# A two-layer attention and expert kernel: first operands chunk by chunk, chunks in natural order, three score banks, routing inside the loop, gathers in smaller groups

## What is computed

```python
# layer 0: s = linear attention by running sums, g = x @ ternary weights + bias
# layer 1 attention (16 heads of 16), over all rows of its batch, causal:
qkv = hidden_states @ qkv_w.T + qkv_b
scores = einsum('bqhd,bkhd->bhqk', q, k) * scale + slope[h] * (key - query)
attn = softmax(where(key <= query, scores, NEG))
out = (attn @ v) @ out_w.T + out_b
# layer 1 experts: the best 2 of 8 for each row
logits = x @ gate_w.T + gate_b
top_vals, top_idx = top_k(logits, 2); routing = softmax(top_vals)
for e in range(8):
    h = x @ w1[e].T + b1[e]
    y = h[:, 0::2] * sigmoid(1.702 * h[:, 0::2]) * (h[:, 1::2] + 1)
    out += (y @ w2[e].T + b2[e]) * weight_of(e)
```

## Time and profile before

| what | value |
|---|---|
| median of 3 runs | 972.3 us (968.9 to 974.0) |
| profiled execution, its own time | 969.48 us |
| its span, first to last instruction | 967.7 us |
| mean granted TensorE clock | 0.923 |
| PE, DVE, ACT, POOL busy | 796.4, 635.3, 498.7, 313.9 us |

### The profile page before, as it was taken

One profiled execution on the slowest core, in us unless ns is written; L12 is line 12 of the kernel. 1 busy time (PEld: TensorE's weight loads), 2 busy tenths in 40 slices (PEclk: granted clock), 3 DMA queues, 4 the chain that ended last, 5 costly groups with the idle time before them and its releaser, 6 DMA issues.

```text
span 967.7 us, 13783 instructions
## 1 busy us (share of the span) xinstructions
PE 796.4 (82%) x4910; PEld 387.1 (40%) x4910; DVE 635.3 (66%) x1197; ACT 498.7 (52%) x1030; POOL 313.9 (32%) x363
## 2 busy tenths in 40 slices
PE   4474659914889999999999999999999995888986
PEld 1242345403324444444544444444444432222543
DVE  5999997665856666676566667666666763984121
ACT  2343315861555565555555655555565552556340
POOL 2766963121660060051006005100600516340111
PEclk9797979966799999999999999999999997999795
DMA  9501302332223235225223532522353112111110
GB/s 322 173 0 66 109 22 87 131 108 70 102 93 88 67 99 100 76 63 107 62 66 103 101 73 65 106 62 66 98 108 71 40 49 77 45 55 68 42 34 33
DMA packets 72392, 80.03 MB, mean 83 GB/s; under 512 B 33561, under 2 KB 56020, under 8 KB 72196
## 3 DMA queue, kind: packets, MB, share of 16 engines
q1 hardware_dynamic: 67660, 68.84, 26.0%
q0 software_dynamic: 3296, 8.62, 2.9%
q10 hardware_dynamic: 1368, 1.70, 0.6%
HBM read 34.22 MB, written 26.74 MB: 63 GB/s over the span
## 4 chain that ended last, share of the span: by engine, by line
PE 55%; DVE 26%; issue 7%; POOL 3%; DMA 3%; ACT 3%; SPq 1%; POOLq 0%; ACTq 0%; DVEq 0%
PE bank L1466 14%; DVE PM L1163 11%; PE bank L1424 10%; PE bank L1444 7%; PE bank L1361 5%; PE bank L1371 5%; PE bank L1481 3%; DVE PR L960 3%; PE bank L1256 2%; PE bank L1508 2%; DMA OPS<-qk_parts 2%; DVE YT L1062 2%; POOL XT L580 1%; POOL x_rows L569 1%; PE bank L1427 1%
## 5 line engine op out<-in xcount | busy, mean ns | idle before, releaser
L1163 DVE TENSOR_REDUCE PM<-bank 128x1 f32<-128x512 f32 (+3 forms) x640 | 368.6, 605 | 217.7 <-PE bank L1427 160.1
L811 ACT ACTIVATE PR<-bank 128x512 f32<-128x512 f32 (+3 forms) x640 | 331.6, 536 | 302.7 <-PE bank L1447 150.7
L1424 PE MATMUL bank<-OPS 108*128 108x512 bf16 (+3 forms) x640 | 228.5, 361 | 72.3 <-DVE PM L1163 36.1
L1444 PE MATMUL bank<-OPS 111*128 111x512 bf16 (+3 forms) x640 | 225.0, 354 | 3.3 <-ACT PR L811 3.1
L1466 PE MATMUL bank<-PR,VS 128*17 128x512 f32 (+3 forms) x1280 | 159.0, 548 | 0.5 <-ACT PR L811 0.4
L540 POOL TENSOR_TENSOR NP<-NM,NIL 128x8 bf16<-128x8 f32 x32 | 6.5, 202 | 429.9 <-DVE NM L1171 429.8
L1424 PEld LDWEIGHTS bank<-OPS 108*128 108x128 bf16 x640 | 64.2, 100 | 193.3 <-DVE PM L1163 131.9
L1361 PE MATMUL bank<-WB 128*128 128x256 f16 x552 | 90.7, 272 | 0.0
L527 POOL TENSOR_TENSOR OPS<-POSR,SCL 12x2048 bf16<-12x2048 bf16 x24 | 87.8, 3680 | 7.6 <-PE bank L1447 7.6
L1444 PEld LDWEIGHTS bank<-OPS 111*128 111x128 bf16 x640 | 63.3, 99 | 39.0 <-ACT PR L811 15.6
L1361 PEld LDWEIGHTS bank<-WB 128*128 128x128 f16 x552 | 49.5, 99 | 44.6 <-issue 22.3
(11 more groups left out here) (187 smaller groups left out, 975.8 us busy)
## 6 DMA issues: line engine op xcount, KB each, us to landing
qk_parts<-OPS SPq DMA_DIRECT2D x16, 384.0 KB, 3.6
OPS<-qk_parts SPq DMA_DIRECT2D x32, 192.0 KB
x_rows<-PR SPq DMA_DIRECT2D x23, 256.0 KB, 3.6
WB<-W1H SPq DMA_DIRECT2D x23, 256.0 KB, 2.4
WB<-W1L SPq DMA_DIRECT2D x23, 256.0 KB, 2.4
WB<-in_w SPq DMA_DIRECT2D x23, 256.0 KB, 2.7
y_rows<-XT SPq DMA_DIRECT2D x23, 256.0 KB, 2.2
OPS<-qk_parts SPq DMA_DIRECT2D x32, 128.0 KB
```

The costliest lines, as they stand in the source:

```text
L811: act.activation(PR[:, tile % RING, off:CH], PS[2 + tile % 2][:, off:CH], ACT.Exp).then_inc(b_exped, 1)
L1163: dve.tensor_reduce(PM[:, c % 2, j, xq, gg:gg + 1], bank[:, 0:width], AX.X, ALU.max).then_inc(a_reduced, 1)
L1424: last = mm(bank[:, 0:width], OPS[0:ROWS_A, h % 4, 0, P * (TC * a + xq):P * (TC * a + xq) + P], OPS[0:ROWS_A, h % 4, 1, CH * gg:CH * gg + ...
L1444: last = mm(bank[:, off:CH], OPS[0:ROWS_B, h % 4, 1, P * k:P * k + P], OPS[0:ROWS_B, h % 4, 0, CH * b + off:CH * b + CH], start=True, stop ...
```

## The change

The chunk order becomes 0, 1, 2, 3, with 8, 16, 24 and 32 tiles: a pair's chunks end at places 7, 23, 47 and 79, and every turn comes five steps later (places 12, 28, 52, 4). The parts of queries and keys move to memory outside the operand region OPS, and SP stores each chunk and then loads that chunk of heads 0 and 1 (twelve transfers a chunk) instead of loading whole rows at the end; heads 2 and 3 stay as they were. Before PE's first tile of a chunk in pair 0 there is now a wait for that chunk alone. The position rows of heads 0 and 1 move from ACT to POOL, ahead of the last two experts' weight scaling. The ranking becomes five operations on 1024 elements a partition, and the whole routing (36 operations, two a step) runs in steps 1 to 18 of the loop, the turning of the weights and the bias products in steps 19 to 41. After the first 44 tiles the first pass uses three banks (0, 1, 6), and PE waits for the reduction of tile n - 3. Both halves of `up` use bank 5: the second half starts nine steps after the first and waits for DVE's reading of the first; `down` comes 18 steps after the start, blocks start at step 92. The scatters go in groups of 4, 8 and 4 tiles, the gathers in groups of 3, 5 and 8. POOL's list around `rows` is not touched.

```diff
-ORDER = (0, 3, 1, 2)
+ORDER = (0, 1, 2, 3)
-FIRST_BLOCK, EVERY = 84, 20
+FIRST_BLOCK, EVERY = 92, 20
-TURN_AT = {chunk_end(m) - 1 + (3, 4, 5, 3)[m % NC]: m for m in range(NC * PAIRS)}
-HEADS_AT = {chunk_end(m) - 1 + LEAD + (15, 11, 11, 11)[m % NC]: m for m in range(NC * PAIRS)}
+TURN_AT = {chunk_end(m) - 1 + 5: m for m in range(NC * PAIRS)}
+HEADS_AT = {chunk_end(m) - 1 + LEAD + 11: m for m in range(NC * PAIRS)}
-DOWN_AT = {n + 14: b for n, b in BLOCK_AT.items()}
+DOWN_AT = {n + 18: b for n, b in BLOCK_AT.items()}
+BIAS_AT = {19 + 2 * k: k for k in range(NC + NT // 2)}
...
-            load(0)
-            load(1)
+            for c in range(NC):
...
+                sp.wait_ge(parts_out[0], 16 * c + 16)
+                sp.wait_ge(parts_out[2], 16 * c + 16)
+                for h in range(2):
+                    for side in range(2):
...
+                            sp.dma_start(OPS[row:row + rows, h, side, cols], src).then_inc(first_in[c], 16)
...
+            rows(0)
+            rows(1)
+            scale(E // 2 - 1)
+            pool.wait_ge(w1l_done, E - 2)
+            low_parts(E // 2 - 1)
...
-            scatter(range(0, 5))
+            scatter(range(0, 4))
             maxima(1)
-            scatter(range(5, 11))
+            scatter(range(4, 12))
             maxima(2)
-            scatter(range(11, NT))
+            scatter(range(12, NT))
             maxima(3)
...
-                    gather(0, GATHERS)
+                    gather(0, 3)
                 maxima(NC * p)
                 if p == PAIRS - 1:
-                    gather(GATHERS, 11)
+                    gather(3, 8)
                 maxima(NC * p + 1)
                 if p == PAIRS - 1:
-                    gather(11, NT)
+                    gather(8, NT)
                 if 1 <= p < PAIRS - 1:
                     pool.wait_ge(b_scored, PER_PAIR * p)
                     rows(2 * p + 2)
...
-                    if b == 0:
-                        pe.wait_ge(slots_done, 2)
-                    else:
-                        pe.wait_ge(y_ready, 2 * b + f - 1)
+                    wait(pe, y_ready, 2 * b + f)
-                last = mm(PS[5 + f][:, SLOTS * part:SLOTS * part + SLOTS], W1B[b % 2][:, wp, col:col + P],
+                last = mm(PS[5][:, SLOTS * part:SLOTS * part + SLOTS], W1B[b % 2][:, wp, col:col + P],
...
+                if p == 0 and tile == OFF[c]:
+                    pe.wait_ge(first_in[c], 16 * 12)
...
-                    pe.wait_ge(a_reduced, tile - 1)
-                bank = PS[tile % 4] if tile < WIDE else PS[tile % 2]
+                    pe.wait_ge(a_reduced, tile - 2)
+                bank = PS[tile % 4] if tile < WIDE else PS[(0, 1, 6)[tile % 3]]
```

The new ranking, first of 36 operations of `sort(k)`, two of which DVE does after each reduction:

```diff
+                if k == 0:
+                    ins = dve.tensor_tensor(RIVAL, other, own, ALU.is_gt)
+                elif k == 1:
+                    ins = dve.tensor_tensor(EQUAL, other, own, ALU.is_equal)
...
+                elif k == 4:
+                    ins = dve.tensor_reduce(RANK, RIVAL, AX.X, ALU.add)
...
+                if 1 <= n <= SORTED // 2:
+                    sort(2 * n - 2)
+                    sort(2 * n - 1)
```

More of the change, by code:

```diff
@@ L351, in _ @@
                 sp.dma_start(x1_dram[:, TC * c:TC * c + TC, :], XO[:, TC * c:TC * c + TC, :]).then_inc(x1_spill, 16)
-            with sp.Fori(0, NC) as c:
-                for m in range(4):
-                    side, half = m // 2, m % 2
-                    sp.wait_ge(qk_p2, 4 * c + m + 1)
-                    sp.dma_start(parts[side, :, half * P:half * P + P, ds(c * CH, CH)].rearrange("j f t -> f j t"),
-                                 QP[:, m, :, :]).then_inc(parts_out[m], 16)
             def load(h):
@@ L378, in rows_out @@
                         "j (q t) -> j q t", q=TC), MT[3 * TC * j:3 * TC * j + 3 * TC, m % 2, :]).then_inc(mrow[m % NC], 16)
-            for m in range(4):
-                sp.wait_ge(parts_out[m], 16 * NC)
-            load(0)
-            load(1)
+            for c in range(NC):
+                cols = slice(CH * c, CH * c + CH)
+                for m in range(4):
+                    side, half = m // 2, m % 2
+                    sp.wait_ge(qk_p2, 4 * c + m + 1)
+                    sp.dma_start(parts[side, :, half * P:half * P + P, cols].rearrange("j f t -> f j t"),
+                                 QP[m]).then_inc(parts_out[m], 16)
+                sp.wait_ge(parts_out[0], 16 * c + 16)
+                sp.wait_ge(parts_out[2], 16 * c + 16)
+                for h in range(2):
+                    for side in range(2):
+                        row = POS
+                        for first, parts_of, times_of in LOADS[side]:
+                            rows = HD * parts_of * times_of
+                            src = parts[side, first:first + parts_of, HD * h:HD * h + HD, cols]
+                            if times_of > 1:
+                                src = src.broadcast_to([times_of, HD, CH])
+                            sp.dma_start(OPS[row:row + rows, h, side, cols], src).then_inc(first_in[c], 16)
+                            row += rows
             sp.wait_ge(memset_done, 11)
@@ L387, in _ @@
                              ONEB[0:3, :].unsqueeze(1).broadcast_to([3, NC, CH])).then_inc(ones_in, 16)
+            for m in range(4):
+                sp.wait_ge(parts_out[m], 16 * NC)
             load(2)
@@ L721, in _ @@
                     wait(act, parts_out[m], 16 * c)
-                    act.activation(QP[:, m, 0, :], QV[:, m, :], ACT.Copy).then_inc(qk_p0, 1)
+                    if c == 0 and m == 2:
+                        act.wait_ge(x1_add, 2 * NC)
+                    act.activation(QP[m][:, 0, :], QV[:, m, :], ACT.Copy).then_inc(qk_p0, 1)
                 if c + 1 < NC:
@@ L746, in gate_linear @@
                 half = slice(SLOTS * f, SLOTS * f + SLOTS)
[L747 removed]
+                act.activation(GT[:, b % 2, half], PS[5][:, 0:SLOTS], ACT.Identity,
                                bias=BB[:, b % 2, 0, f:f + 1]).then_inc(gate_read, 1)
@@ L1117, in slots @@
-            def slots(k):
-                if k == 0:
-                    dve.wait_ge(count_ps, 1)
-                    dve.wait_ge(table_in, 16)
-                    dve.wait_ge(we_done, 2)
-                else:
-                    dve.wait_ge(chain, k)
-                if k == 0:
+            over = TMP.rearrange("p t e -> p (t e)")[:, 0:8 * E].rearrange("p (e j) -> p e j", e=E)
+            own = LG[:, :, :].unsqueeze(3).broadcast_to([P, NT, E, E])
+            other = LG[:, :, :].unsqueeze(2).broadcast_to([P, NT, E, E])
@@ L1403, in output_biases @@
                     tile = 2 * r + q
-                    last = mm(PS[4 + r % 2][:, D * q:D * q + D], WET[:, P * tile:P * tile + P], B2[:, :],
+                    last = mm(PS[4 + r % 2][:, D * q:D * q + D], WET[0:E, P * tile:P * tile + P], B2[0:E, :],
                               start=True, stop=True)
@@ L1512, in _ @@
             pe.wait_ge(cast_in, 32)
-            side_work = [(turn_routing, c) for c in range(NC)] + [(output_biases, r) for r in range(NT // 2)]
             for n in range(STEPS):
@@ L1516, in _ @@
                     score_a(n)
-                    if n % 2 and n // 2 < len(side_work):
-                        stage, which = side_work[n // 2]
-                        stage(which)
-                if n == 1:
+                    if n in BIAS_AT:
+                        if BIAS_AT[n] < NC:
+                            turn_routing(BIAS_AT[n])
+                        else:
+                            output_biases(BIAS_AT[n] - NC)
+                if n == 5:
                     count_tokens()
```

247 lines of the change are left out of this document (124 added, 123 removed).

## The result

The changed kernel takes 995.9 us (median of 4, 993.9 to 999.6) where the kernel before takes 972.8 (median of 4, 968.9 to 974.0): a ratio of 1.025, 95% interval 1.021 to 1.029. It is slower by 23 us. The forecast was 1013 us, slower, with a range of 988 to 1038: the side and the range held, the size was 17 us too large. The profiled execution took 993.9 us with a span of 992.1, against 969.5 and 967.7 before.

The account below looks back on a forecast made before the run. In-order PE bounds the loop and its waits are paid in full. Stalls +52, clock +18, banks and gate work -5, start -10, gathers -12, tail +0.5 make +43.5 on 969.5: 1013 us, range 988 to 1038.

Parts of the forecast that it names:

- the main step: Turn at place 52, pairs 1 to 6: PE waits 8.7 us a pair for POOL's unchanged list, 52 us in all.
- The rival with the loads: Third chunk's maxima at place 68, behind next pair's loads: some 5 us late, hidden by the stall at place 52; 4%.
- The 995 us: Total time given for late loads taking about half of the stall's place, if POOL were not late; 4%.
- The clock: After each stall in pairs 1 to 6: slow granted clock loses 3.0 us, ends 1.5 and 4.5; 18 us over six.
- The six dips: Sign in the new profile: the granted clock dips six times, beside six waits of the turns for POOL.
- Banks and gate work: Third score bank and `up` in one bank, in the pairs: net -0.8 us a pair, -5 over six, ends -18 and +10.
- bank 7: Places 10, 12, 28, 30, 50 and 52, where `down` and turns come two steps apart: +1.0 us a pair (0.7 to 1.5).
- Start: Projections to step 52: loads by chunk, routing in the loop; first tile about 202, step 52 at 259; -10, ends -18 and 0.
- a first tile after 210: Sign at the start that would make the forecast wrong at its second step; the first tile was expected near 202.
- The ranking itself: Routing on DVE between the first reductions: five ranking operations 5.3 us, others 9, POOL's lock 6; sum 20, ends 14 and 24.
- Gathers and tail: Last pair: six gathers instead of twelve ahead of the turn, 10.23 us stall goes, -12 (-8 to -14); tail +0.5.
- the sum of 43.5: Whole kernel: all terms added, slower by 43.5 us than the profiled execution's 969.5, giving 1013 us.

Follow-up runs that it names:

- e1: Changed kernel with POOL doing the third chunk's maxima before the next pair's position rows: 959.6 us, -10.3 against the kernel before (0.989).
- e2: Changed kernel with the third chunk turned at place 60 instead of 52, POOL's list as it is: 970.9 us, +1.0 against the kernel before (1.000).
- e5: e1 with the loads of the next pair's second head issued behind the third chunk's turned rows: 967.7 us, -19.9 against the kernel before (0.980).
- e12: e6 with the second head's loads one step later, behind the block fetch at place 54: 930.1 us, -41.9 against the kernel before (0.956).
- e9: Changed kernel with the old chunk order (0, 3, 1, 2), that chunk's heads four steps later, gathers three and eight: 981.1 us, +9.7 against the kernel before (1.014).
- e10: e9 with two banks instead of three for first-pass tiles from tile 44 on: 1004.2 us, +32.7 against the kernel before (1.038).
- e7: e5 with two banks instead of three for first-pass tiles from tile 44 on: 1026.2 us, +38.6 against the kernel before (1.039).
- e6: e5 with the position rows of heads 0 and 1 made by ACT instead of POOL: 959.5 us, -28.1 against the kernel before (0.973).
- e11: e9 with the position rows of heads 0 and 1 made by ACT instead of POOL: 971.2 us, -0.2 against the kernel before (1.001).
- e8: Kernel before with the last pair's gathers spread, three and eight tiles instead of six and five: 984.8 us, -2.8 against the kernel before (0.996).

## Why the prediction was right, and where its sizes were off

**What bounds the loop, and the main step: right.** PE in order, POOL's list fixed, third chunk's turn eight places too early. Forecast from place 43 to the turn: 16.7 us; measured 16.6 and 16.7. It was forecast as one wait of 8.7; it came as 2.86 for DVE and 3.7 for POOL on average ((24.8 - 2.5) / 6), with the rest in PE's own work at half the clock. So the turns' waits are 2.9 to 5.3 us and the pair 91.8, where the text looked for 7 to 9.5 and 94 to 97. e1 shows the cause: with the maxima first the pair becomes 6.4 us shorter. It took away both waits at once; e2, which moves the turn and leaves the rows where they are, frees only the turn's, so the wait for DVE is a second cause, not forecast, inside the time that POOL's list sets.

**The rival with the loads: right in mechanism, at its place, and hidden as the text said.** It was to be seen only if POOL were not late, at about 5 us a pair. e1 uncovers it: 2.9 us of wait at place 68, and 3.2 us of period when e5 removes it. With both gone the pair is 91.8 - 82.2 = 9.6 us shorter; the forecast had 8.7 + 3.0 for stall and clock. The 995 us that the text gives for this rival do not follow from its own terms: 1013 - 52 - 18 and 6 x 5 for the loads are 973.

**The clock: about right on average.** The granted clock in the 75 us behind the stall was 0.97 and 0.94, so 4.5 and 9 us of them at 1.2 GHz instead of 2.4 (an estimate from the two levels), a loss of 2.2 and 4.6 against 3.0 forecast. The six dips are there, three of them down to 0.50 for the 8 us behind the turn (pairs 2, 4 and 6) and three at 0.72 to 0.74.

**Banks and gate work: the term that was furthest off.** The forecast took the waits of a tile for DVE, 4.4 us a pair, as the most that a third bank could give. It set half of that, 2.3, and took 1.5 back for bank 7 and ACT: 0.8 was left. Freed of stall and loads, the pair is 81.1 us at the full clock (e12) instead of 84.5: -3.4. Over pairs 1 to 6 that is 16 us more than forecast, and the last pair has its share too; by size this is most of the error of 17 us. The bound of 4.4 was right, the choice inside it wrong. In the steady pairs the tiles wait no more for DVE, so the whole 4.4 went (PE's waits in a free pair of e12 are for ACT alone), and bank 7 cost less than the 1.0 set for it: the waits of the turns for ACT are 0.9 us a pair in e12 (4.4 in five pairs), where they were 0.7. The bank alone was measured as 3.5 us a pair (e9, e10), with `glu` held up in both, and at about 2.3 by the estimate under e7. How the rest divides between the bank and the even spread of `up` was not tried. The larger miss is one that the forecast had no term for: which DVE operations fall beside POOL's rows when the steps shift. It decides about more than the bank does (e7, e12).

**Start: -10 forecast, -1.9 measured.** Right: the loads by chunk fit beside the projections, and no tile waited for them. Wrong: the price of POOL's rows ahead of the weights. The text had named a first tile after 210 as the sign that this step is wrong, and it came at 213. I had looked at who needs POOL's next product (ACT, 3.2 us), and not at what runs on DVE beside the rows. The same text priced this very collision for the ranking, from the earlier trace rows, at 1.19 us against 0.28; there the POOL operation was 1.16 us long. For rows of 3.7 us the same rule gives 3.7 us for every DVE operation with two SBUF operands that meets them. Four did so (L1048, 13.95 us for four that take 2.8 alone), and the runs put the loss at 8.2 and 9.9 us (e6, e11). The trace agrees with the Trainium skill (SBUF — State Buffer, Who interferes with whom), which has a DVE instruction with two SBUF inputs contend with a GpSimd instruction that reads SBUF, calls the contention an exclusive lock, and lets the order of issue decide who waits. The ranking itself came out near its sum: step 19 (L1414) stands 27.5 us behind the first tile, forecast 30, with 12.5 of them as one wait at `count_tokens`. Step 52 is at 272 instead of 259, later by the 11 us of the first tile and 2 more.

**Gathers and tail: -11.5 forecast, about -17 measured.** From the rows of pair 6 to the end the kernel gained 10.1 us, although that stretch holds the sixth stall, by which the average pair is 7.3 us longer. Of the 17.4 us that this makes some 3.4 would be the third bank, if the last pair gained by it as the steady ones did. The wait in the last pair is 2.47 us instead of 10.23, and the tiles' waits for DVE there 2.8 instead of 7.5. Alone, on its chip, the edit gave 1 to 7 us (e8), so the share of the gathers stays open.

**The errors cancelled in part.** By pieces: the start 8 us too low, the five pairs 18 too high, the end 9.5 too high; together about the 19 us between the sum of 43.5 and the 24.4 of the spans.

## What to carry to other kernels

When a consumer is moved earlier in a fixed schedule, walk through every queue that feeds it, POOL's list and SP's as well, and move the producer by as much. Fix the first one and look for the next: here turn, then loads, then a transpose behind the loads, each hidden by the one before. And price a long POOL operation by up to its whole duration for each DVE operation with two SBUF operands beside it. Giving it to ACT paid here (e6, e11); cutting it into short ones was not tried. A comparison of two versions can turn on such a meeting alone, so look for it in both traces before you name the cause.

## What the runs showed of the hardware

- An unlucky DVE operation lasts as long as POOL's: `glu` 0.41 to 0.43 us alone, 3.64 to 3.69 beside row operations of 3.6 us; L1048 0.69 alone, 8.09 for two beside them. It can also be POOL that waits: 3.88 us for the fourth row operation in e12 where `glu` came first. Which of the two happens can hang on 0.2 us (e12).
- The price of a short wait of PE can be more than double its length, and it is not fixed: in e12 one wait of 3.12 us, then 8.7 us at a granted clock of 0.50, and a pair that is 7.8 us longer than its neighbours; in e6 the same wait of 3.12 us, a clock of 1.00 behind it, and a pair about 2 us longer.
- Two transfers of 3 KB took 15 us from issue to use behind twelve loads (e1), and a transpose took 6.0 us to issue behind six of them (e6), against 1.3 ahead of them (e12).
- Chips differ by stretch, not by a factor: on one, the kernel before took 15 to 18 us more, and its pairs without scatters or gathers were as long as elsewhere (84.5 us in e8).
